# Local attention scores with one head per matmul: 64 rows by 32 columns, head halves interleaved on the partitions

## The chip, the cores and the metric

The kernel runs on one core of one Trainium2 chip. The metric is the device time in microseconds of one execution. The core has TensorE (PE, with its weight loads shown as PEld), VectorE (DVE), ScalarE (ACT), GpSimd (POOL) and SyncE (SP), which here only issues transfers.

## The reference

The input x is float32, 4 batch entries of 512 tokens with 128 features. Two sublayers follow each other, each with a residual and a layer norm at its end. The first is full attention with 16 heads of 8 features and an ALiBi bias. The second is a stack of six local layers, and the change is in their attention:

```python
for i in range(6):
    x = attn_layer(shift_tokens(x), Wqkv[i], q_scale[i], k_scale[i], Wo[i]) + x
    x = ffn_layer(shift_tokens(x), ln_g[i], ln_b[i], W1[i], b1[i], W2[i], b2[i]) + x
# attn_layer: 16 heads of 64 features; q and k are normalized, scaled and rotated
q = l2norm(q) * qs                     # the same for k
q = q * cos * scale + rotate_half(q) * sin * scale
# local_attention: windows of 32 queries; each sees its own window and the one before
sim = einsum('bhwie,bhwje->bhwij', bq, bk2) * 8.0      # bk2: 64 keys for each window
sim = where(mask, -max, sim)           # mask: j < i, or j > i + 32, or no such key
out = einsum('bhwij,bhwje->bhwie', softmax(sim), bv2)
```

`rotate_half` mixes feature d with feature d + 32 of a head, so a head's 64 features are held as two halves of 32. All work is float32.

## The kernel before

The program has four parts in sequence: the first attention (`alibi_attention`), a product of value and output weights for each head (`fold_values`), the six local layers (`local_layers`) and the last norm. The local layers take about three quarters of the time.

In `local_layers` a unit is one batch entry in one layer (24 units), and a unit has four quarters of four heads each (GH = 4), 96 quarters in all. Every engine runs the same loop `step(s)` over s, with its own part of the work written out in order by hand; semaphores join them. In step s the engines project and rotate k and q of quarter n = s, compute the scores of quarter c = s - 1, the exponentials of quarter d = s - 2, and weigh the rows of quarter e = s - 3; quarter h = s - 4 is projected out. Once per unit, spread over the steps, the feed-forward part runs: transposes, gate and linear matmuls (`first_half`, L902), GELU (L1015, with a table load at L1010 before it), the product hid (L1215), its second matmul (L986).

TensorE's order within one step is: k projection (L862), projection out (L881), q projection (L862), `weigh_rows` (L873), the sum over each head's features for k (L946), `scores` (L894), the same sum for q (L956), then the unit's feed-forward matmuls and transposes (L907).

The other engines follow. VectorE multiplies the projections by scale and rotation tables (L1135 to L1142), transposes the probabilities (L1156), floors the sums (L1178, L1196), sums the exponentials (den, L1181), inverts (rden, L1184), adds the mask to the scores (s_in, L1188 and L1190) and takes the row maximum (s_max, L1200). ScalarE squares the projections (L1026, L1031, L1037, L1039), takes the exponentials (L1001, 16 of 128x64 per step), copies the weighed rows zT out of PSUM (L997) and takes logarithm and exponential of the sums. POOL adds the squares (sumk, L1090; sumq, L1096), finishes the rotation in qfin and kfin (L1099, L1100, L1104, L1105), multiplies s_max by rq (lower, L1110) and normalizes the probabilities (L1078).

`qfin` and `kfin` hold on partition 32 hh + d the features d (index 0) and d + 32 (index 1) of head hh. The scores contract over 128 partitions, so transfers rearrange them: `qpair[:, p]` gets heads 2p and 2p + 1, each half of the features in one half of the partitions. `kpad` has the same rows but one copy for each of the two heads e, in which the other head's partitions stay zero; so one matmul of 128 rows gives both heads' scores for 32 queries and 2 x 64 keys. It has one leading window of zeros. The four windows w of a tile of 128 tokens go to PSUM partitions 32w to 32w + 31, that is to four 32-column strips of the array.

SyncE issues the transfers of quarter n in step s = n: four for `qpair` (L832) after `qfin_ok`, eight for `kpad` (L839) after `kfin_ok`, all behind a wait for the scores of quarter n - 1, then the rows `xk_prev` and the next weights. `bank_z` is PSUM of four banks: the scores use banks 0 and 1, which the weighed rows z of quarter e used before; hence the scores wait for `z01_ok`, the first of the two copies to zT. `pT` holds the transposed probabilities in the order t (tile of 128 tokens), then head; `rq` and `prob` use the same order.

## Time and profile before

| | us |
|---|---|
| median of 3 runs | 2041.87 |
| lowest and highest run | 2039.39, 2042.81 |
| the profiled execution, device time | 2042.99 |
| the profiled execution, span of the trace | 2040.9 |

The span runs from the first to the last instruction of the profiled execution; its device time is longer by 2.1 us. The profile was taken once, so durations from it are those of one execution. TensorE's mean granted clock is 0.968 of full speed over the span.

A group of rows names a source line, an engine, what is written and read, and the shapes. The x behind a group is its count. A float32 matmul of the program leaves two matmul and two weight load records. Idle time in brackets is that of the engine ahead of the instruction, with what ended it. Busy time of matmuls that run side by side counts once.

Loop steps repeat in a pattern of four, one unit. The rows below are taken from one such pattern, whose steps are called A (1013.83 to 1029.80 us, from one k projection to the next), B (to 1047.85), C (to 1063.96) and D (to 1078.07). By the code's order A has the gate matmuls, B the GELU and the linear matmuls, C the second matmul of the feed-forward part and D transposes and the norm's scaling.

### The profile page before, as it was taken

The page shows a single profiled execution, that of the slowest core. Times are in us where ns is not written, and L with a number is a line of the kernel's source. Part 1 is how long each engine was busy: PE and PEld are TensorE (multiplying, and loading weights), DVE is VectorE, ACT ScalarE, POOL GpSimd, SP SyncE. Part 2 cuts the span into 40 slices and gives each one's busy share as a digit, 9 for nine tenths or more (in the row PEclk, how much of TensorE's full clock was granted, in tenths as well). Part 3 has the DMA queues.
Part 4 walks back from the last instruction along what each step waited for, and adds up shares of the span by engine and source line. Part 5 has one row for each costly group of instructions (what it writes and reads, how often), then busy time and mean ns, then how long its engine had stood idle before and what let it go on. Part 6 is the DMA issues. An engine that isn't in the chain of part 4 may idle for free. (4 is left out here: it accounts for less than half of the span.)

```text
span 2040.9 us, 47434 instructions
## 1 busy us (share of the span) xinstructions
PE 1835.3 (90%) x18048; PEld 1023.9 (50%) x18048; DVE 1544.4 (76%) x2543; ACT 1383.9 (68%) x2862; POOL 1263.2 (62%) x1127
## 2 busy tenths in 40 slices
PE   5898898668999999999999999999999999999984
PEld 3443344524555555555555555555555555555541
DVE  4778886257877788788887888878887788877753
ACT  1454445237777777877778777778777877778851
POOL 4303300057877777777777787777877778777721
PEclk8899999769999999999999999999999999999996
DMA  9000000215323343233432234332343322233300
GB/s 192 2 2 1 2 2 2 63 46 98 75 69 75 81 89 75 68 71 82 87 80 69 68 81 86 74 79 68 75 88 74 83 68 69 67 77 84 71 22 21
DMA packets 142992, 131.86 MB, mean 65 GB/s; under 512 B 85160, under 2 KB 88808, under 8 KB 142440
## 3 DMA queue, kind: packets, MB, share of 16 engines
q1 hardware_dynamic: 142768, 128.83, 28.4%
q8 instruction: 145, 2.38, 0.5%
q14 instruction: 79, 0.65, 0.1%
HBM read 20.94 MB, written 1.05 MB: 11 GB/s over the span
## 5 line engine op out<-in xcount | busy, mean ns | idle before, releaser
L1001 ACT ACTIVATE prob<-s_in,lower,rq 128x64 f32<-128x64 f32 x1536 | 537.9, 430 | 79.0 <-POOL lower L1110 77.0
L862 PE MATMUL bank_a<-x_shift,wqk_sb 128*128 128x512 f32 x768 | 375.2, 612 | 69.1 <-ACT sq L1031 57.5
L881 PE MATMUL bank_y<-zT,wvo 128*128 128x512 f32 x768 | 345.2, 592 | 0.0
L1090 POOL TENSOR_TENSOR sumk<-sq 128x512 f32<-128x512 f32 x96 | 122.3, 1274 | 271.6 <-ACT sq L1031 271.6
L862 PEld LDWEIGHTS bank_a<-x_shift,wqk_sb 128*128 128x128 f32 x768 | 140.1, 193 | 262.0 <-issue 148.4
L881 PEld LDWEIGHTS bank_y<-zT,wvo 128*128 128x128 f32 x768 | 146.0, 190 | 183.7 <-issue 183.7
L894 PEld LDWEIGHTS bank_z<-kpad,qpair 128*32 128x32 f32 x6144 | 164.6, 110 | 100.1 <-issue 98.8
L894 PE MATMUL bank_z<-kpad,qpair 128*32 128x128 f32 x6144 | 187.7, 274 | 23.2 <-ACT zT L997 23.2
L491 DVE TENSOR_REDUCE a_negmax<-a_max 128x1 f32<-128x512 f32 x256 | 164.7, 685 | 47.9 <-PE a_max L166 44.3
L382 ACT ACTIVATE a_prob<-a_sT 128x1024 f32<-128x1024 f32 x128 | 130.5, 1023 | 103.7 <-PE a_sT L216 101.8
L997 ACT ACTIVATE zT<-bank_z 128x1024 f32<-128x1024 f32 x192 | 186.1, 1023 | 10.7 <-PE bank_z L873 8.0
L1078 POOL TENSOR_TENSOR prob<-prob,rden 128x1024 f32<-128x1024 f32 x96 | 182.9, 1905 | 3.9 <-DVE rden L1184 3.9
L1096 POOL TENSOR_TENSOR sumq<-sq 128x512 f32<-128x512 f32 x96 | 122.0, 1270 | 92.5 <-ACT sq L1039 92.5
L873 PE MATMUL bank_z<-pT,xk_prev 32*128 32x128 f32 x3072 | 164.8, 284 | 3.2 <-DVE xn L1162 1.7
L873 PEld LDWEIGHTS bank_z<-pT,xk_prev 32*128 32x128 f32 x3072 | 122.4, 187 | 78.4 <-issue 56.1
L873 PE MATMUL bank_z<-pT,xk_own 32*128 32x128 f32 x3072 | 154.8, 271 | 0.0
L1135 DVE SCALAR_TENSOR_TENSOR pk<-bank_a,scale_sb,rot_sb 128x512 f32<-128x512 f32 x96 | 71.8, 748 | 104.3 <-PE bank_a L862 94.3
L461 POOL TENSOR_TENSOR a_rstd<-a_mv,eps 128x4 f32<-128x4 f32 x4 | 0.8, 198 | 232.8 <-DVE a_mv L549 232.8
L1099 POOL TENSOR_TENSOR qfin<-pq 128x512 f32<-128x512 f32 x96 | 123.7, 1289 | 0.0
L873 PEld LDWEIGHTS bank_z<-pT,xk_own 32*128 32x128 f32 x3072 | 123.0, 188 | 0.0
L1141 DVE SCALAR_TENSOR_TENSOR pk<-bank_a,scale_sb,rot_sb 128x512 f32<-128x512 f32 x96 | 71.6, 746 | 67.6 <-ACT sq L1026 67.6
L1104 POOL TENSOR_TENSOR kfin<-rk,pk 128x512 f32<-128x512 f32 x96 | 122.1, 1272 | 0.5 <-ACT rk L1050 0.5
(161 smaller groups left out, 3947.3 us busy)
## 6 DMA issues: line engine op xcount, KB each, us to landing
qpair<-qfin SPq DMA_DIRECT2D x384, 128.0 KB, 2.3
kpad<-kfin SPq DMA_DIRECT2D x768, 64.0 KB, 2.0
wqk_sb<-in_wqkv SPq DMA_DIRECT2D x24, 256.0 KB, 5.6
xk_prev<-xk_own SPq DMA_DIRECT2D x24, 192.0 KB, 2.4
ffn_sb<-in_ffn SPq DMA_DIRECT2D x6, 537.5 KB, 3.9
wv_in<-in_wqkv SPq DMA_DIRECT2D x12, 256.0 KB, 4.8
wo_in<-in_wo SPq DMA_DIRECT2D x6, 512.0 KB, 5.8
xk_prev<-xk_own SPq DMA_DIRECT2D x24, 48.0 KB, 2.1
```

What stands on the lines that cost most here:

```text
L382: act.activation(prob[:, j % 2, 2 * half:2 * half + 2, :], sT_bank[:, 2 * half:2 * half + 2, :], ACT.Exp).then_inc(exp_ok, 1)
L491: dve.tensor_reduce(negmax[:, unit // 4, unit % 4:unit % 4 + 1], max_bank[u % 2][:], AX.X, ALU.max, negate=True).then_inc(max_ok, 1)
L862: last = pe.matmul(bank_a[:, half, :], wqk_sb[:, layer_of(u) % 2, part, half, g * P:(g + 1) * P], cols(u), start=True, stop=True)
L873: last = pe.matmul(bank_z[:, w, t * P:(t + 1) * P], rows[at, u % 2, t, :], pT[at, n % 2, c, t * GH:(t + 1) * GH, :].rearrange("p h q -> p ...
L881: last = pe.matmul(bank_y[:].rearrange("p (t w q) -> p t w q", w=WPT, q=WIN), wvo[:, layer_of(u), GH * g + hh, :], zT[:, n % 2, :, :, hh, ...
L894: last = pe.matmul(bank_z[WIN * w:WIN * w + WIN, t // 2, c:c + P], qpair[:, p, at:at + WIN], kpad[:, p, :, at:at + 2 * WIN], start=True, s ...
L997: return act.activation(out, in_, ACT.Copy)
L1001: last = act.activation(prob[:, n % 2, i, :], s_in[:, n % 2, i, :], ACT.Exp, bias=lower[:, n % 2, i:i + 1], scale=rq[:, n % 2, i:i + 1])
L1078: pool.tensor_tensor(prob[:, e % 2], prob[:, e % 2], rden[:].unsqueeze(2).broadcast_to([P, TPB * GH, 2 * WIN]), ALU.mult).then_inc(pn_ok, 1)
L1090: pool.tensor_tensor(sumk[:], sq[:, 0, :], sq[:, 1, :], ALU.add).then_inc(sumk_ok, 1)
L1099: pool.tensor_tensor(qfin[:, 0, :], pq[:, 0, :], pq[:, 1, :], ALU.subtract)
L1104: pool.tensor_tensor(kfin[:, 0, :], rk[:], pk[:, 0, :], ALU.mult)
```

## The change

The zero padding of heads goes away. `kpad` loses its head index; `qpair` and `kpad` get one head e on each half of the partitions, its two feature halves interleaved on even and odd partitions. Each score matmul takes one head: 64 rows by 32 columns and 64 keys, the two heads of a pair go to different banks. There are twice as many score matmuls with half the keys each. The order of heads in the scores, and so in `pT`, the sums for q and the masks, becomes head within pair, tile, pair; `weigh_rows` and `project_out` pick their columns accordingly. SyncE moves q and k by halves, two transfers each for the first and the second feature half, and the first half waits only for the first of POOL's two products (new semaphores `qfin0_ok`, `kfin0_ok`): eight transfers in place of twelve.

```diff
--- before.py
+++ after.py
@@ -739,7 +739,7 @@
         kfin = sb("kfin", [P, 2, L])
         qfin = sb("qfin", [P, 2, L])
         qpair = sb("qpair", [P, 2, L])
-        kpad = sb("kpad", [P, 2, 2, WIN + L])
+        kpad = sb("kpad", [P, 2, WIN + L])
         s_in = sb("s_in", [P, 2, TPB * GH, 2 * WIN])
         s_max = sb("s_max", [P, TPB * GH])
         lower = sb("lower", [P, 2, TPB * GH])
@@ -777,6 +777,7 @@
         sumk_ok, sumq_ok, rotk_ok, kfin_ok, qfin_ok, pn_ok, eps_ok, rstd_ok = map(
             sem, ["sumk_ok", "sumq_ok", "rotk_ok", "kfin_ok", "qfin_ok", "pn_ok", "eps_ok", "rstd_ok"])
         kpad_in, qpair_in, prev_in = sem("kpad_in"), sem("qpair_in"), sem("prev_in")
+        qfin0_ok, kfin0_ok = sem("qfin0_ok"), sem("kfin0_ok")
 
         def after(eng, s, n, each=1):
 
@@ -825,19 +826,17 @@
                     after(sp, xf_ok, B * layer + B - 1)
                     sp.dma_start(ffn_sb[:], ffn[layer + 1]).then_inc(ffn_loaded, 16)
                 if quarter(n):
-                    after(sp, qfin_ok, n)
                     after(sp, s_mm, n - 1)
-                    for p in range(2):
-                        for half in range(2):
-                            sp.dma_start(qpair[64 * half:64 * half + 64, p, :],
+                    for half, ok in ((0, qfin0_ok), (1, qfin_ok)):
+                        after(sp, ok, n)
+                        for p in range(2):
+                            sp.dma_start(qpair[half:P:2, p, :],
                                          qfin[64 * p:64 * p + 64, half, :]).then_inc(qpair_in, 16)
-                    after(sp, kfin_ok, n)
-                    for hh in range(GH):
-                        p, e = hh // 2, hh % 2
-                        for half in range(2):
-                            to = 64 * half + 32 * e
-                            sp.dma_start(kpad[to:to + 32, p, e, WIN:WIN + L],
-                                         kfin[32 * hh:32 * hh + 32, half, :]).then_inc(kpad_in, 16)
+                    for half, ok in ((0, kfin0_ok), (1, kfin_ok)):
+                        after(sp, ok, n)
+                        for p in range(2):
+                            sp.dma_start(kpad[half:P:2, p, WIN:WIN + L],
+                                         kfin[64 * p:64 * p + 64, half, :]).then_inc(kpad_in, 16)
                 u = rows_at(s)
                 if u is not None:
                     after(sp, xk_ok, u)
@@ -871,7 +870,7 @@
                         for w in range(WPT):
                             at = slice(WIN * w, WIN * w + WIN)
                             last = pe.matmul(bank_z[:, w, t * P:(t + 1) * P], rows[at, u % 2, t, :],
-                                             pT[at, n % 2, c, t * GH:(t + 1) * GH, :].rearrange("p h q -> p (h q)"),
+                                             pT[at, n % 2, c].rearrange("k (e t p) q -> k t e p q", e=2, t=TPB)[:, t],
                                              start=(c == 0), stop=(c == 1), skip_group_check=True)
                 last.then_inc(z_mm, 1)
 
@@ -879,7 +878,7 @@
                 u, g = divmod(n, GROUPS)
                 for hh in range(GH):
                     last = pe.matmul(bank_y[:].rearrange("p (t w q) -> p t w q", w=WPT, q=WIN),
-                                     wvo[:, layer_of(u), GH * g + hh, :],
+                                     wvo[:, layer_of(u), GH * g + 2 * (hh % 2) + hh // 2, :],
                                      zT[:, n % 2, :, :, hh, :].rearrange("p w t q -> p t w q"),
                                      start=(g == 0 and hh == 0), stop=(g == GROUPS - 1 and hh == GH - 1),
                                      skip_group_check=True)
@@ -889,12 +888,12 @@
                 for t in range(TPB):
                     for p in range(2):
                         for w in range(WPT):
-                            at = t * P + w * WIN
-                            c = (t % 2) * 2 * P + p * P
-                            last = pe.matmul(bank_z[WIN * w:WIN * w + WIN, t // 2, c:c + P],
-                                             qpair[:, p, at:at + WIN],
-                                             kpad[:, p, :, at:at + 2 * WIN], start=True, stop=True,
-                                             skip_group_check=True)
+                            for e in range(2):
+                                at, rows = t * P + w * WIN, slice(64 * e, 64 * e + 64)
+                                c = t * P + p * 2 * WIN
+                                last = pe.matmul(bank_z[WIN * w:WIN * w + WIN, e, c:c + 2 * WIN],
+                                                 qpair[rows, p, at:at + WIN], kpad[rows, p, at:at + 2 * WIN],
+                                                 start=True, stop=True, skip_group_check=True)
                 last.then_inc(s_mm, 1)
 
             def first_half(out, u, half, j):
@@ -945,7 +944,7 @@
                     after(pe, floorq_ok, n - 1)
                     pe.matmul(bank_f[:], same_head[:], sumk[:], start=True, stop=True).then_inc(sumk_mm, 1)
                 if quarter(c):
-                    after(pe, kpad_in, c, 128)
+                    after(pe, kpad_in, c, 64)
                     after(pe, qpair_in, c, 64)
                     after(pe, z01_ok, min(c - 2, QUARTERS - 1))
                     scores(c)
@@ -953,7 +952,7 @@
                     after(pe, sumq_ok, n)
                     after(pe, floor_ok, n)
                     for t in range(TPB):
-                        last = pe.matmul(bank_f[:, t * GH:(t + 1) * GH], sumq[:, t * P:(t + 1) * P], pick_head[:],
+                        last = pe.matmul(bank_f[:, 0:TPB * GH].rearrange("q (e t p) -> q t e p", e=2, t=TPB)[:, t], sumq[:, t * P:(t + 1) * P], pick_head[:],
                                          start=True, stop=True, skip_group_check=True)
                     last.then_inc(sumq_mm, 1)
                 if quarter(e):
@@ -1096,12 +1095,12 @@
                     pool.tensor_tensor(sumq[:], sq[:, 0, :], sq[:, 1, :], ALU.add).then_inc(sumq_ok, 1)
                     after(pool, pq_ok, n)
                     after(pool, qpair_in, n - 1, 64)
-                    pool.tensor_tensor(qfin[:, 0, :], pq[:, 0, :], pq[:, 1, :], ALU.subtract)
+                    pool.tensor_tensor(qfin[:, 0, :], pq[:, 0, :], pq[:, 1, :], ALU.subtract).then_inc(qfin0_ok, 1)
                     pool.tensor_tensor(qfin[:, 1, :], pq[:, 2, :], pq[:, 3, :], ALU.add).then_inc(qfin_ok, 1)
                     after(pool, rk_ok, n)
                     after(pool, rotk_ok, n)
-                    after(pool, kpad_in, n - 1, 128)
-                    pool.tensor_tensor(kfin[:, 0, :], rk[:], pk[:, 0, :], ALU.mult)
+                    after(pool, kpad_in, n - 1, 64)
+                    pool.tensor_tensor(kfin[:, 0, :], rk[:], pk[:, 0, :], ALU.mult).then_inc(kfin0_ok, 1)
                     pool.tensor_tensor(kfin[:, 1, :], rk[:], pk[:, 2, :], ALU.mult).then_inc(kfin_ok, 1)
                 if quarter(c):
                     after(pool, max_ok, c)
@@ -1116,7 +1115,7 @@
             pool.wait_ge(prev_zero, 1)
             for hh in range(GH):
                 pool.memset(same_head[32 * hh:32 * hh + 32, 32 * hh:32 * hh + 32], 1.0)
-                last = pool.memset(pick_head[32 * hh:32 * hh + 32, hh:hh + 1], 1.0)
+                last = pool.memset(pick_head[32 * hh:32 * hh + 32, 2 * (hh % 2) + hh // 2:2 * (hh % 2) + hh // 2 + 1], 1.0)
             last.then_inc(const_ok, 1)
             for s in range(STEPS_ALL):
                 step(s)
@@ -1189,7 +1188,7 @@
                                       mask_sb[:], ALU.add)
                     dve.tensor_tensor(s_in[:, c % 2, 8:16, :],
                                       bank_z[:, 1, :].rearrange("p (h n) -> p h n", n=2 * WIN),
-                                      mask_sb[:, 4:5, :].broadcast_to([P, 8, 2 * WIN]), ALU.add).then_inc(mask_ok, 1)
+                                      mask_sb[:], ALU.add).then_inc(mask_ok, 1)
                 if quarter(n):
                     after(dve, sumq_mm, n)
                     after(dve, lnq_ok, n - 1)
@@ -1222,7 +1221,7 @@
                     dve.scalar_tensor_tensor(hi, bank_z[64:P, 3, :], b2_sb[64:P], hi, ALU.add,
                                              ALU.add).then_inc(xf_ok, 1)
 
-            dve.memset(kpad[:].rearrange("p a b n -> p (a b n)"), 0.0).then_inc(kpad_zero, 1)
+            dve.memset(kpad[:].rearrange("p a n -> p (a n)"), 0.0).then_inc(kpad_zero, 1)
             dve.wait_ge(const_in, 16 * 18)
             for s in range(STEPS_ALL):
                 step(s)
@@ -1338,7 +1337,7 @@
     ok = (j >= i) & (j <= i + WIN)
     first = ok & ~((np.arange(P)[:, None] < WIN) & (j < WIN))
     low = np.float32(-(2.0 ** 100))
-    return np.stack([np.where(m, np.float32(0), low) for m in [first] * GH + [ok] * GH], 1).astype(np.float32)
+    return np.stack([np.where(m, np.float32(0), low) for m in [first] * 2 + [ok] * 6], 1).astype(np.float32)
 
 
 def three_parts(a):
```

## Rows read from the trace of the kernel before

**Rows 1.** Busy time of each engine over the span, part 1 of the page.
```profile
PE 1835.3 (90%) x18048; PEld 1023.9 (50%) x18048; DVE 1544.4 (76%) x2543; ACT 1383.9 (68%) x2862; POOL 1263.2 (62%) x1127
```

**Rows 2.** Busy time by windows: step B, and the sum over steps A to D.
```profile
1029.80:1047.85 18.05, 15.77 (x162) 8.72 (x160) 12.58 (x18) 14.09 (x31) 11.88 (x11) 1.00 0.26 60
...
sum 64.24, PE 61.34 PEld 35.22 DVE 52.22 ACT 50.19 POOL 49.06; mean PE 15.34 PEld 8.81 DVE 13.05 ACT 12.55 POOL 12.27
```

**Rows 3.** All waits of PE from 600 to 1900 us: total, times, longest.
```profile
PE bank_a L862 <- ACT sq L1031: 37.4, 20, 1.9
PE bank_z L894 <- ACT zT L997: 19.1, 81, 0.4
```

**Rows 4.** Windows, L894 alone: length, PE, PEld, clock, transfers.
```profile
1024.30:1024.40 0.10, 0.06 (x4) 0.09 (x8) 1.00 0.00 0
1024.30:1026.30 2.00, 1.96 (x64) 1.72 (x64) 1.00 0.00 0
```

**Rows 5.** Windows, L873 alone, the weighing of rows in step A.
```profile
1021.03:1021.06 0.03, 0.02 (x4) 0.02 (x4) 1.00 0.33 68
1021.03:1023.20 2.17, 2.07 (x64) 1.88 (x64) 1.00 0.45 125
```

**Rows 6.** Timeline around the scores in step B, then in step D.
```profile
1044.40 0.69 DVE L1188 TENSOR_TENSOR s_in<-bank_z,mask_sb 128x512 f32<-128x512 f32 x1 [0.28 <-PE bank_z L894]
...
1074.36 1.96 PE L894 MATMUL bank_z<-kpad,qpair 128*32 128x128 f32 x64 [0.18 <-ACT zT L997]
...
1076.07 0.25 DVE L1184 RECIPROCAL rden<-den 128x16 f32<-128x16 f32 x1
...
1076.38 0.69 DVE L1188 TENSOR_TENSOR s_in<-bank_z,mask_sb 128x512 f32<-128x512 f32 x1
```

**Rows 7.** Timeline from a step D into step A.
```profile
1008.90 1.27 POOL L1096 TENSOR_TENSOR sumq<-sq 128x512 f32<-128x512 f32 x1 [1.39 <-ACT sq L1039]
...
1015.05 0.23 POOL L1110 TENSOR_TENSOR lower<-s_max,rq 128x16 f32<-128x16 f32 x1
...
1018.46 0.58 ACT L1031 ACTIVATE sq<-bank_a 128x512 f32<-128x512 f32 x1
...
1019.12 0.30 PEld L862 LDWEIGHTS bank_a<-x_shift,wqk_sb 128*128 128x128 f32 x2 [0.81 <-ACT sq L1031]
```

**Rows 8.** Timeline at the end of step A and the start of B.
```profile
1028.33 1.28 ACT L1010 ACT_TABLE_LOAD   x1
...
1028.94 1.02 PE L902 MATMUL bank_f<-xnT,ffn_sb 128*85 128x512 f32 x2
...
1030.00 0.68 ACT L1015 ACTIVATE hid<-bank_f,ffn_sb 85x512 f32<-85x512 f32 x1 [0.39 <-PE bank_f L902]
```

**Rows 9.** Timeline at the start of step C.
```profile
1048.05 1.41 DVE L1215 SCALAR_TENSOR_TENSOR hid<-bank_z,ffn_sb,hid 128x512 f32<-128x512 f32 x2 [1.10 <-PE bank_f L902]
```

**Rows 10.** Timeline of VectorE from step C into step D.
```profile
1063.50 0.38 DVE L1209 BATCH_NORM_AGGREGATE mv<-stats 128x2 f32<-128x6 f32 x4
...
1064.16 0.74 DVE L1221 SCALAR_TENSOR_TENSOR x_shift<-bank_z,ffn_sb,x_shift 64x512 f32<-64x512 f32 x1 [0.28 <-PE bank_z L986]
...
1065.88 0.75 DVE L1135 SCALAR_TENSOR_TENSOR pk<-bank_a,scale_sb,rot_sb 128x512 f32<-128x512 f32 x1 [0.20 <-PE bank_a L862]
...
1069.68 1.32 DVE L1162 TENSOR_SCALAR xn<-bank_z,mv,rstd 128x128 f32<-128x128 f32 x4
...
1071.03 0.75 DVE L1135 SCALAR_TENSOR_TENSOR pq<-bank_a,scale_sb,rot_sb 128x512 f32<-128x512 f32 x1
```

**Rows 11.** Transfers: issues on the page, SP's wait, one timeline row.
```profile
qpair<-qfin SPq DMA_DIRECT2D x384, 128.0 KB, 2.3
kpad<-kfin SPq DMA_DIRECT2D x768, 64.0 KB, 2.0
...
SPq L784 <- PE bank_z L894: 581.4, 81, 9.9
...
1015.15 5.02 SPq L839 DMA_DIRECT2D kpad<-kfin  x8
```

## The prediction

> **What bounds the kernel now.** I read the page's busy shares first. TensorE is busy 90% of the span, far ahead of the other engines [rows 1], so a shorter block of matmuls could count. The busy share is an average, so I went to the local layers, where the change is. One loop step handles one quarter (four heads of one batch entry), and the four steps A to D repeat as a pattern of 64.24 us [rows 2]. TensorE is busy 61.34 of these 64.24 us at the full granted clock (1.00, 2.4 GHz). Its list of waits has two entries, over 81 steps: the q projection waits for ScalarE's Square in 20 of them, 37.4 us together, and the scores wait for the zT copy, 0.24 us each time [rows 3]. The reader should see that TensorE idles 2.9 us in 64 and nearly sets the pace, but that ScalarE already sets it in one step of four.
>
> **The score block itself.** It is 64 matmul records (a float32 matmul leaves two) and as many weight loads, 1.96 us busy, of which 1.72 us lie between the first and the last weight load [rows 4]. That is 0.1075 us for each four, one on each 32-column strip: 258 cycles of 2.4 GHz for 128 keys. So a strip takes two cycles for a key, and four strips run side by side. The block is bound by the columns that stream, not by issue. The weighting block shows the same for the other direction: 32-row tiles, 64 records in a stretch of 2.07 us busy, four of them started within 0.03 us [rows 5]. So tiles that differ in columns run together and tiles that differ in rows run together, in different banks.
>
> **The change, part by part.**
>
> *Half the columns, twice the matmuls.* Before, a matmul contracts 128 rows and computes two heads' keys, half of the products with padding zeros. After, 64 rows and 64 keys: 128 records, each with half the stream (0.054 us), on eight tiles (two row halves, four strips), whose order alternates halves, each half writing its own bank. If all eight run together the block is 128/8 x 0.054 = 0.86 us from first to last start, against 1.72. The tail behind the last start (1.96 - 1.72 = 0.24) shrinks by 0.05; against that, I allow 0.1 us for the first round, whose 16 instructions must arrive one by one. I take 1.16 us for the block, a gain of **0.80 us** per step on TensorE.
>
> *Can instructions arrive fast enough?* No stretch of this trace needs more than four pairs in 0.107 us for long. From above: in the first 0.10 us of the block eight loads and four matmuls had started, the first load 0.09 us before the window's end [rows 4]. Loads and matmuls alternate in the program, so the eighth load is the 15th instruction: 6 ns each at most. At 6 ns, 256 instructions take 1.54 us and the gain is 0.18 us. From below: 27 ns per pair, the average of both blocks, would be a floor if the chip issued matmuls no faster than that; the block would be 128 x 0.027 = 3.44 us, a loss of 1.72 us. The bursts [rows 4, 5] are the nearest evidence, four pairs in 0.03 us, so I take the fast case as likeliest.
>
> *Where the 0.80 us go.* The scores' end releases VectorE's masking (L1188). But VectorE does den and rden before it and ends them at 1076.32; the masking starts at 1076.38, and the scores ended at 1076.32 too [rows 6]. The two are level, in steps A, C and D; in B the masking waits 0.28 us. So masking, and the row maximum behind it, gain nothing. Only the matmuls behind the scores on TensorE's own queue start earlier. I follow each stretch from one q projection to the next.
>
> D to A: POOL runs without a gap from the sum for q (1008.90) over qfin and kfin to lower (1015.05), then ScalarE's exponentials and Squares run to 1019.04, and the q projection's weights, loaded from 1019.12, had waited 0.81 us for that Square [rows 7]. No score is in this chain. Gain **0**.
>
> A to B: the gate matmuls end earlier, but GELU needs its table first: the table load ends at 1029.61 and GELU started at 1030.00, released by TensorE [rows 8]. At most 0.39, less 0.05 of handover. ScalarE is then busy up to the next q projection. Gain **0.34**.
>
> B to C: the linear matmuls release VectorE's product for hid, for which it sat idle 1.10 us [rows 9]; everything up to the projection follows. Gain **0.80**.
>
> C to D: VectorE ends the aggregate at 1063.88 and its add (L1221) waited 0.28 us for TensorE. It can start 0.25 earlier, and the next product (L1135), which waited another 0.20 us for the k projection, 0.45 in all. From there VectorE runs without a gap up to xn, which ends at 1071.00, and the q products follow at 1071.03 [rows 10]. The projection gains 0.80, but what it releases gains 0.45. Gain **0.45**.
>
> Sum: 0.34 + 0.80 + 0.45 = 1.59 us in four steps. By the loop, GELU steps come every fourth step from step 11, 22 of them before the last quarter, so 22 such groups: 22 x 1.59 = **35 us**. In the first eight steps there is no feed-forward work, the chain of D to A rules, and I count nothing.
>
> *The transfers.* Eight instead of twelve issues per step, each of 64 partitions. They landed 2.0 and 2.3 us after issue [rows 11]. SP's queue waits 581 us for score matmuls in 81 steps, which is room, not cost. The last kpad issue ends at 1020.17 and the scores that read it start at 1024.3 [rows 4, 11], so the cover is 2 us even after landing. The first halves can start one POOL product (about 1.27 us) earlier and are behind the same wait for the previous scores. The new waits stand on SP alone, ahead of the next transfers and xk_prev, which also has slack. POOL's and VectorE's counts are unchanged, the signals ride on instructions that exist. Cost 0; if the cover were gone, a step would pay at most one landing, 2.3 us.
>
> *The rest.* Reordered columns of pT, wvo, pick_head and the masks, and the unbroadcast mask, keep the sizes; a strided stream of 64-column pieces was already the scores' form. Cost 0.
>
> **The sum.** The profiled run took 2042.99 us (span 2040.9 and 2.1 around it): 2042.99 - 35.0 = 2008.0. It lies 1.1 above the median of 2041.87, so I predict **2007 us**.
>
> **Rivals.**
>
> *1. Partly fed.* The stream of 256 instructions, not the array, sets the block: 6 ns each gives a gain of 0.18 us, worth 0.18 x 3 in four steps (A to B, B to C, C to D), 22 x 0.54 = 12 us: 2030 us. For it: the block starts behind a wait in every step [rows 3], so its instructions aren't all queued up. Against: it is an upper bound on the spacing. Anything between 2007 and 2030 belongs here.
>
> *2. Weight loads share a path.* If the four strips of a row half load one after the other at 0.027 us each (32 columns, two cycles), they take 0.107 us per eight, and the block stays at 1.72: no change, 2042 us. The present block can't exclude it by its average. Against: eight loads, two for each strip, started in 0.09 us [rows 4], where one path would give 0.22.
>
> *3. Issue bound, slower.* Matmuls are issued at a floor of 27 ns per pair in a long stream, the bursts being only what a full queue hands over. Then the block is 3.44 us, +1.72 on TensorE's own queue in each of 96 steps, 165 us: about 2207 us. For it: both blocks average 27 to 29 ns per pair, though one is tiled by rows and one by columns. Against: both have the same stream per tile and four tiles, which explains the same number. It decides from 13.4 ns per pair (1.72/128) upwards; at 18 ns, between that and 27, the block grows by 0.58 us and the kernel ends near 2098.
>
> The Trainium skill speaks for this rival: "TensorE: Matmul & The Clock Gate", in the section on 56 against 53.3 ns, says that starts of matmuls never come closer than about 25 ns however small they are. By that rule the block would be 128 x 0.025 = 3.2 us and the kernel, with +1.48 in 96 steps, would take about 2184 us. This trace shows starts within a burst closer than that, on different tiles, and an average just above it.
>
> *4. Clock.* With TensorE idle more, its clock could drop. It stays at 1.00 in B, where the idle wait is 1.87 us [rows 2, 3]; idle stretches grow by under 1 us. I give it nothing of its own.
>
> **Chances.** The fast case (2000 to 2015) 0.58; partly fed, 2015 to 2037, 0.10; no change, by rival 2 or a balance of both, 0.08; slower, 0.24, half of it below 2100. A change within 0.2% (4 us) can't be told from none. Faster 0.68, same 0.08, slower 0.24. The range runs from 1988, where the bounds by VectorE and POOL would be too strict and half as much again is gained, to 2098; about 0.14 lie outside. The likeliest case's own range is 1998 to 2015.
>
> **What would show it.** Right: a score block near 1.15 us with twice the records; the scores-to-masking gap opening by 0.8 us and masking released by rden; TensorE waiting for ScalarE in the q projection of A too; GELU released by its table load; step lengths that shrink by 0.8 in B to C and not in D to A; transfers with no waiter. Wrong: a block above 1.72 us with pair starts spaced evenly over it (rival 3), or rounds of eight at 0.107 us (rival 2); masking that does start earlier would make the gain larger than 35 us.

## The result, and the profile after

| | median, us | lowest to highest | runs |
|---|---|---|---|
| before | 2042.28 | 2039.39 to 2042.81 | 5 |
| after | 2029.19 | 2028.43 to 2030.77 | 5 |

The ratio is 0.994, with a 95% interval of 0.9926 to 0.9955: the kernel is 13.1 us faster. The forecast was 2007 us, a gain of 35. The sign is right, the gain is well under half of what I predicted, and the time lies outside the likeliest case's own range. The profiled execution took 2030.68 us, with a span of 2028.9 us and a mean granted clock of 0.963 (before 0.968).

New line numbers are one lower than those of before: the projections are L861, the scores still L894, the masking L1187, the Square L1030.

The page's busy times [rows 1], and the queue that fetches instructions. Its columns are packets, MB, and the share of 16 engines' span.

```profile
PE 1800.8 (89%) x24192; PEld 992.7 (49%) x24192; DVE 1529.0 (75%) x2543; ACT 1380.8 (68%) x2862; POOL 1262.7 (62%) x1127
```

```profile
q8 instruction: 194, 3.18, 0.6%
```

TensorE has 6,144 more matmul records and is busy 34.5 us less. The second line is one that I hadn't shown of before, where it reads 145 packets and 2.38 MB. Each packet is 16 KB. With its semaphore waits TensorE executes about 49,600 instructions where it executed 37,300, so there is about one packet to 256 of them.

Busy time by windows of the score block, L894 alone, in a step D (columns as in [rows 4], which show a block of step A; the block of step D before is in [rows 6]):

```profile
1074.50:1074.60 0.10, 0.05 (x8) 0.08 (x12) 1.00 0.00 0
1074.50:1076.10 1.60, 1.48 (x128) 1.34 (x128) 1.00 0.00 0
```

The block takes 1.48 us, where it took 1.96 and I had said 1.16. It gives each step 0.48 us, not 0.80.

The same view by steps, with all instructions: A, B and the sum over A to D, one pattern of four later than that of [rows 2]:

```profile
1077.78:1093.75 15.97, 15.29 (x226) 8.35 (x225) 12.28 (x17) 13.89 (x31) 13.58 (x12) 1.00 0.47 106
1093.75:1111.32 17.57, 15.30 (x225) 8.35 (x224) 12.43 (x18) 14.15 (x31) 11.88 (x11) 1.00 0.28 60
...
sum 62.81, PE 59.43 PEld 33.73 DVE 51.62 ACT 50.01 POOL 49.06; mean PE 14.86 PEld 8.43 DVE 12.90 ACT 12.50 POOL 12.26
```

Four steps shrank from 64.24 to 62.81 us. Between the q projections, as medians over the 22 groups, C to D went from 16.11 to 15.63, D to A stayed at 14.29, A to B went from 17.82 to 17.34, and B to C from 16.02 to 15.54: 0.48, 0, 0.48 and 0.48 us, together 1.44. Twenty-two times 1.44 is 31.7 us. Less than half of that reached the kernel's time: 13.1 us.

TensorE's waits from 600 to 1900 us show why (total, times, longest):

```profile
PE bank_a L861 <- ACT sq L1030: 45.1, 37, 1.9
PE bank_z L894 <- ACT zT L996: 19.3, 82, 0.4
PE bank_z L894 <- issue: 6.3, 3, 2.1
PE bank_z L906 <- issue: 2.6, 3, 1.1
PE bank_z L901 <- issue: 2.2, 2, 1.3
PE bank_f L955 <- issue: 1.6, 1, 1.6
```

The first two are those of [rows 3]. The Square is now waited for in 37 places, not 20. The four lines "issue" are new: time in which TensorE waited for nothing that the profile knows. Nine waits hold 12.7 us, and three of them are inside the score block. The timeline of one:

```profile
684.23 1.31 PEld L894 LDWEIGHTS bank_z<-kpad,qpair 64*32 64x32 f32 x125 [0.98 <-issue]
684.26 1.44 PE L894 MATMUL bank_z<-kpad,qpair 64*32 64x64 f32 x125 [0.18 <-ACT zT L996]
...
687.69 0.14 PEld L894 LDWEIGHTS bank_z<-kpad,qpair 64*32 64x32 f32 x3 [2.15 <-issue]
687.69 0.30 PE L894 MATMUL bank_z<-kpad,qpair 64*32 64x64 f32 x3 [1.99 <-issue]
...
688.03 0.69 DVE L1187 TENSOR_TENSOR s_in<-bank_z,mask_sb 128x512 f32<-128x512 f32 x1 [1.81 <-PE bank_z L894]
...
690.53 2.77 PE L861 MATMUL bank_a<-x_shift,wqk_sb 128*128 128x512 f32 x4
```

After 125 of its 128 pairs the block stops for 2.2 us, with everything that the last three read long in place. VectorE's masking stands idle for it, 1.81 us. And the projection behind it takes 2.77 us instead of 1.88. The windows show the reason, in the column of the granted clock:

```profile
684.20:685.50 1.30, 1.24 (x125) 1.27 (x125) 1.30 (x2) 1.30 (x2) 1.30 (x2) 1.00 0.05 13
685.50:687.65 2.15, 0.20 (x21) 0.04 (x5) 0.68 (x2) 0.67 (x2) 2.15 (x3) 1.00 0.00 0
687.70:690.50 2.80, 2.80 (x19) 2.71 (x20) 2.47 (x4) 1.03 (x3) 1.52 (x2) 0.71 0.46 99
690.50:693.30 2.80, 2.80 (x7) 1.29 (x6) 0.07 (x1) 2.45 (x7) 2.08 (x2) 0.68 0.95 206
```

The clock had been at 1.00 (2.4 GHz). After the gap it is granted 0.71 and 0.68, a mixture with 1.2 GHz, so the gap costs more than itself.

The same stretch in the transfer view, whose 40 slices are 0.125 us each:

```profile
GB/s 0 0 0 0 0 0 0 0 0 0 131 0 0 0 0 0 0 0 0 0 0 0 0 0 0 0 0 0 0 0 0 0 0 0 0 0 0 0 0 0
...
q8 instruction: 1, 0.02, 1.2%
```

The window is 684 to 689 us, and the one packet in it is an instruction packet: it begins in slice 11, at 685.35, 1.1 us into the block. By its record it takes 0.96 us, and TensorE goes on 1.38 us after its end.

Counting every TensorE instruction of the trace, waits included, I find eight gaps of over 1 us that no semaphore explains:

| quarter | 16 | 26 | 31 | 72 | 77 | 82 | 87 | 92 |
|---|---|---|---|---|---|---|---|---|
| gap, us, from start to start | 2.21 | 2.36 | 2.33 | 1.42 | 1.04 | 1.59 | 1.26 | 1.87 |
| place | in the block | in | in | behind it | behind | behind | behind | behind |

All eight begin at the same place of a 256-instruction grid: the first instruction behind the gap has a count that leaves 193 when divided by 256. They add up to 14.1 us. The stretches that they lie in, with the slower clock behind them, exceed the median of their kind by 20.2 us. And 31.7 - 20.2 = 11.5 us, against 12.0 by which the span became shorter. Of these 12.0, 1.4 lie ahead of the first q projection of the local layers, where the change does nothing, so the account closes to between one and two microseconds.

So two things had to be explained: the block's 1.48 us, and the gaps. My theory from here on: (a) the score block is bound by the arrival of its 256 instructions, 1289 ns from first to last start, or 5.0 ns each; (b) TensorE's instructions come in blocks of 256, and when 256 of them are used up faster than the next block can be fetched, TensorE stands still. The rivals: the array itself, or row halves that exclude each other, set the block; and the gaps belong to some event of those quarters (a weight reload, a busy port), not to the instruction count.

### The profile page after: what moved, and what is told of

Same layout as the page of the kernel before. It is cut to its first block and busy times, and to the rows that moved or that the text cites. A ratio compares the mean times of both kernels' runs of the same rounds, so it can differ in the third digit from the quotient of the medians.

```text
span 2028.9 us, 59338 instructions
## 1 busy us (share of the span) xinstructions
PE 1800.8 (89%) x24192; PEld 992.7 (49%) x24192; DVE 1529.0 (75%) x2543; ACT 1380.8 (68%) x2862; POOL 1262.7 (62%) x1127
## 5 line engine op out<-in xcount | busy, mean ns | idle before, releaser
L861 PE MATMUL bank_a<-x_shift,wqk_sb 128*128 128x512 f32 x768 | 377.5, 615 | 79.4 <-ACT sq L1030 68.2
L861 PEld LDWEIGHTS bank_a<-x_shift,wqk_sb 128*128 128x128 f32 x768 | 141.7, 195 | 273.3 <-issue 151.4
L894 PEld LDWEIGHTS bank_z<-kpad,qpair 64*32 64x32 f32 x12288 | 129.7, 105 | 107.5 <-issue 107.3
L1095 POOL TENSOR_TENSOR sumq<-sq 128x512 f32<-128x512 f32 x96 | 122.0, 1270 | 94.8 <-ACT sq L1038 94.8
L894 PE MATMUL bank_z<-kpad,qpair 64*32 64x64 f32 x12288 | 143.7, 225 | 29.6 <-ACT zT L996 23.2
L1098 POOL TENSOR_TENSOR qfin<-pq 128x512 f32<-128x512 f32 x96 | 123.5, 1287 | 0.0
L1099 POOL TENSOR_TENSOR qfin<-pq 128x512 f32<-128x512 f32 x96 | 122.3, 1274 | 0.0
```

Of the source, the lines that this page charges most:

```text
L861: last = pe.matmul(bank_a[:, half, :], wqk_sb[:, layer_of(u) % 2, part, half, g * P:(g + 1) * P], cols(u), start=True, stop=True)
L894: last = pe.matmul(bank_z[WIN * w:WIN * w + WIN, e, c:c + 2 * WIN], qpair[rows, p, at:at + WIN], kpad[rows, p, at:at + 2 * WIN], start=Tru ...
L1098: pool.tensor_tensor(qfin[:, 0, :], pq[:, 0, :], pq[:, 1, :], ALU.subtract).then_inc(qfin0_ok, 1)
L1099: pool.tensor_tensor(qfin[:, 1, :], pq[:, 2, :], pq[:, 3, :], ALU.add).then_inc(qfin_ok, 1)
```

## The experiments

Where no number of runs is given, a kernel was run once with a profile, beside a run of the kernel before on the same chip (2042.20 us).

**Half the streamed keys.** It computes only half of the scores (32 of 64 keys in each matmul), with the bank zeroed once; the number of instructions is the same.

```
-  last = pe.matmul(bank_z[WIN * w:WIN * w + WIN, e, c:c + 2 * WIN],
-                   qpair[rows, p, at:at + WIN], kpad[rows, p, at:at + 2 * WIN],
+  last = pe.matmul(bank_z[WIN * w:WIN * w + WIN, e, c:c + WIN],
+                   qpair[rows, p, at:at + WIN], kpad[rows, p, at:at + WIN],
   ...
+  dve.memset(bank_z[:, 0:2, :].rearrange("p w n -> p (w n)"), 0.0)
```

> The changed kernel, but each score matmul takes 32 of its 64 keys, so the stream of each is halved and the number of instructions stays 256 in a block. Half of the scores are left out. Changed kernel: 1.29 us from the first to the last start, 1.50 us busy. Theory 1 (instructions reach TensorE at about 5.0 ns each): the block keeps its 1.27 to 1.30 us between first and last start, and the time stays within 3 us of 2029. Theory 2 (the eight tiles hinder each other, 80 ns for a round of eight matmuls instead of 54): the stream sets the round, the block falls to 0.7 to 0.9 us and the time falls by 10 us or more.

It took 2044.08 us. Its group from 600 to 1900 us:

```profile
L894 PE MATMUL bank_z<-kpad,qpair 64*32 64x32 f32 x10368 | 105.9, 201 | 30.0 <-ACT zT L996 18.2 <-issue 11.8
```

With half the columns the block still needs 1118 ns from first to last start, against 1289: 4.4 ns an instruction. If the columns had set it, it would have halved. But it isn't untouched either: I had expected 1270 to 1300, so the columns have a share of 171 ns, and the arrival of instructions alone doesn't explain the block. The four steps take 62.36 us, 0.45 less than the change's. Yet the time is 15 us worse. There are now 11 gaps, 22.0 us, in stretches that are 35.8 us too long, and five more stretches, without a gap, are 7.0 us too long, because the granted clock fell in them. The faster block uses its instructions up sooner: in quarter 16 the gap starts after 1.08 us of the block and lasts 2.57. My forecast of the time didn't have that.

**Row halves one after the other.** Only the order of the loops differs, so 64 pairs use four tiles and then 64 the other four.

```
-  for t in range(TPB):
-      for p in range(2):
-          for w in range(WPT):
-              for e in range(2):
+  for e in range(2):
+      for t in range(TPB):
+          for p in range(2):
+              for w in range(WPT):
```

> The changed kernel, but all score matmuls of one row half come first and then all of the other, so only four tiles are in use at a time. Nothing else differs. If the two row halves really run side by side in the changed kernel, four tiles with a round of 0.054 us give 128/4 x 0.054 = 1.72 us from first to last start, as before the change, and the time goes back toward 2042. If the halves never overlapped, or if the arrival of instructions alone sets the block, it stays at 1.29 us and 2029.

It took 2075.94 us, and its group from 600 to 1900 us reads:

```profile
L894 PE MATMUL bank_z<-kpad,qpair 64*32 64x64 f32 x10112 | 149.8, 217 | 26.7 <-ACT zT L996 18.5 <-issue 8.2
```

The block needs 1692 ns from first to last start, which is that of four tiles (16 x 107 = 1.72 us). The change's block is shorter than that, so its row halves do run together, and that is where its whole gain is. Four steps take 64.00 us. That the kernel is nevertheless 34 us slower than before is for the most part again the gaps: 9 of them, 14.3 us, in stretches that are 30.3 us too long. Before, 128 instructions took 1.72 us, here 256 do: it isn't the shorter block that brings the gaps, but the larger number of instructions.

Another 10 us are six stretches of 1.7 us too much each that hold no gap. The windows around one of them, ahead of and behind the moment in question:

```profile
905.00:907.90 2.90, 2.79 (x137) 2.73 (x137) 2.87 (x5) 2.02 (x3) 2.90 (x4) 1.00 0.03 6
908.00:911.40 3.40, 3.40 (x5) 1.27 (x5) 1.56 (x3) 1.81 (x3) 3.40 (x4) 0.51 0.78 171
```

TensorE had been busy 2.79 of 2.90 us, with scores and the sum for q, and the granted clock falls from 1.00 to 0.51 all the same. So a wait isn't needed for it; what it takes I can't say.

**Half of the block.** It leaves out the scores of the second half of the query tiles, so each step has 128 instructions fewer; the bank is zeroed once as above.

```
-  for t in range(TPB):
+  for t in range(TPB // 2):
```

> The changed kernel without the score matmuls of the last two of the four token tiles: 64 of 128, half of the scores left out. The block should be 0.65 us between starts. Theory of the prediction (VectorE and POOL set the pace next): D to A stays 14.29 us; A to B and C to D keep the 0.48 us they had gained, within 0.15; B to C falls by another 0.6; with no late instruction fetches the time is about 1995. Rival (TensorE's queue sets the pace throughout): all three stretches fall by 0.6 each, the pattern of four steps is 60.9 us, and the time is about 1969.

It took 2005.71 us, with no gap. The block is 663 ns long, 0.85 us busy. This asks the question that the change was too slow to ask: what would the rest of the kernel make of a really short block? Neither theory came out (1995 and 1969 us). Against before, C to D gained 1.10 us where I had expected 0.48, and D to A lost 0.21, so 0.89 together; A to B gained 0.57. B to C, which should have fallen by another 0.6, gained only 0.18 on average: one stretch of three gained 1.11, and the other two are 0.24 us longer than before. The timeline of the q projection at the start of such a longer stretch, and windows before it and over it, say why:

```profile
1022.16 3.53 PE L861 MATMUL bank_a<-x_shift,wqk_sb 128*128 128x512 f32 x4 [2.40 <-ACT sq L1030]
```

```profile
1016.00:1022.00 6.00, 3.75 (x9) 1.33 (x7) 2.81 (x5) 5.97 (x14) 1.24 (x1) 0.99 0.32 70
1022.16:1025.70 3.54, 3.54 (x8) 1.22 (x8) 2.27 (x3) 2.53 (x8) 3.54 (x3) 0.55 0.00 0
```

TensorE has waited 2.40 us for the Square, longer than the 1.9 us of before, and the granted clock falls from 0.99 to 0.55. The projection takes 3.53 us instead of 1.88, and gives the whole gain of that stretch back. This is my rival 4, which I had given nothing. In the change itself the longest such wait between 600 and 1900 us is 1.9 us, and there the clock fell only behind gaps.

**The count moved by 40.** Ten small matmuls ahead of TensorE's loop, 40 instructions of about 50,000, into a bank that is written afterwards. Nothing in the loop changes but its place on the grid of 256.

```
+  for _ in range(10):
+      pe.matmul(bank_f[0:32, 0:4], ident[0:32, 0:32], ident[0:32, 0:4],
+                start=True, stop=True)
   pe.wait_ge(const_ok, 1)
   for s in range(STEPS_ALL):
```

> The changed kernel with 40 more TensorE instructions (ten matmuls of 32x32 by 4) ahead of its loop, while TensorE waits for POOL anyway. In the changed kernel TensorE ran dry at one place of the score blocks of quarters 16, 26 and 31 (2.2 to 2.4 us each) and a little later in those of 72, 82, 87 and 92; each place is 192 more than a multiple of 256 TensorE instructions. Theory 1 (instructions come in blocks of 256, and a block is asked for too late when the block before is used up in 1.3 us): the gaps leave quarters 16, 26 and 31 and appear in other blocks, in the series 12, 17, 22, 27, 32, always 192 above a multiple of 256. Theory 2 (a transfer or another engine's timing at those moments): the gaps stay in quarters 16, 26 and 31.

It took 2052.59 us, 23 more than the change. TensorE's waits, 600 to 1900 us:

```profile
PE bank_a L861 <- ACT sq L1032: 45.2, 36, 1.9
PE bank_z L894 <- ACT zT L998: 18.9, 80, 0.4
PE bank_z L894 <- issue: 14.0, 7, 2.3
PE bank_f L955 <- issue: 6.3, 4, 2.0
```

The block (1287 ns) and the four steps (62.80 us) are as in the change; the waits for ScalarE are the same too. The gaps are now 13, in quarters 7, 12, 17, 22, 27, 32, 37, 42, 47, 57, 62, 67 and 93, and the three quarters that stopped inside their block in the change (16, 26, 31) run free. All 13 are again at the same place of the grid. The rival that some event in those quarters makes the gap is refuted: the gap follows the count. The account closes again, to a few microseconds: 31.9 us gained by the steps, 41.9 lost in stretches with gaps, together 10.0 slower than before, and 10.4 was measured, although the part ahead of the local layers was 2.9 us faster.

**The count steered.** If the gaps are only a matter of where a block of 256 begins, they can be led away. This one puts 16 small matmuls ahead of the loop, and 11 more in each of four steps, before the sum of k, where the grid would drift back onto the scores.

```
+  for _ in range(11 if n in (34, 50, 66, 82) else 0):
+      pe.matmul(bank_f[0:32, 0:4], ident[0:32, 0:32], ident[0:32, 0:4],
+                start=True, stop=True)
   pe.matmul(bank_f[:], same_head[:], sumk[:], start=True, stop=True)
   ...
+  for _ in range(16):
+      pe.matmul(bank_f[0:32, 0:4], ident[0:32, 0:32], ident[0:32, 0:4],
+                start=True, stop=True)
```

> The changed kernel with dummy matmuls (32x32 by 4, four instructions each) that only move the place of the score blocks in TensorE's instruction stream: 16 ahead of the loop, and 11 ahead of the sum for k in steps 34, 50, 66 and 82. With them no score block from the eighth on starts between 167 and 209 above a multiple of 256, the places at which the blocks of the changed kernel and of shift40 ran dry. Theory 1 (a block of 256 instructions is asked for too late when it is used up in 1.3 us): no gap over 0.3 us inside or right behind a score block is left, the pattern of four steps stays 62.81 us, and the time falls by the 20 us that the late steps add, to 2008 to 2013. Theory 2 (the gaps come about once in so many blocks wherever these stand): gaps of 2 us remain and the time stays at 2025 or above.

| | median, us | lowest to highest | runs |
|---|---|---|---|
| before | 2041.85 | 2038.51 to 2044.69 | 13 |
| steered | 2014.86 | 2013.83 to 2016.57 | 4 |

The ratio to before is 0.9872 (0.9858 to 0.9887): 27.0 us faster than before, about 14 faster than the change. TensorE's waits in the same stretch:

```profile
PE bank_a L861 <- ACT sq L1034: 45.4, 36, 2.0
PE bank_z L894 <- ACT zT L1000: 18.6, 79, 0.4
PE bank_z L906 <- issue: 1.9, 4, 0.7
```

The four steps still take 62.81 us, and no gap is over 1 us. What remains are four waits of up to 0.7 us, in quarters 28, 44, 76 and 92, again at the one place of the grid; I had expected none over 0.3, but the stretches that they lie in are no longer than the median. The cure has its own price: the four A-to-B stretches with 11 more matmuls are 3.0 us longer in all, and in the stretch behind the last of them, after a wait of 2.0 us for the Square, the granted clock fell to 0.50 and cost another 1.4. That is why the time is just above the expected 2013. It is the version that beats both kernels.

**The transfers alone.** The kernel before, with its 12 transfers signalled by halves, so that the first half of qfin and of kfin goes out one POOL product earlier.

```
-  pool.tensor_tensor(qfin[:, 0, :], ...)
+  pool.tensor_tensor(qfin[:, 0, :], ...).then_inc(qfin0_ok, 1)
   ...
-  pool.tensor_tensor(kfin[:, 0, :], ...)
+  pool.tensor_tensor(kfin[:, 0, :], ...).then_inc(kfin0_ok, 1)
   # and on SP's queue, the same for kfin0_ok and kfin_ok
-  after(sp, qfin_ok, n)
   after(sp, s_mm, n - 1)
+  for half, ok in ((0, qfin0_ok), (1, qfin_ok)):
+      after(sp, ok, n)
+      # the transfers of this half
```

> The kernel before the change with one part of it alone: the transfers of qpair and kpad go by halves, the first half after the first of POOL's two products (twelve transfers as before, score matmuls as before). My theory: no engine waits for them, so 2042 within 2 us. Rival: transfers that start earlier let the scores or POOL go on earlier, and part of the 13 us comes from here: 2038 or less.

It took 2041.74 us (2039.68 to 2043.25, 10 runs) against 2041.85, ratio 0.9998 (0.9988 to 1.0008). Earlier transfers are worth nothing, within the measurement's grain. The eight larger transfers of the change weren't run by themselves.

## Why the prediction came out as it did

**The block's size (mis-sized).** The step "I take 1.16 us for the block, a gain of 0.80" is the term that was off: 1.48 us and 0.48. The mechanism was right as far as it went: both row halves do run side by side, since in turn they take 1.69 us. But they don't reach the 0.86 us of eight full tiles, and the best account that I have is that the instructions can't come fast enough to keep them busy. The windows of [rows 4] held the answer, in the figure that I used only as a bound: 6 ns an instruction at most. Measured are 5.0 over the whole block. It isn't even: the first 32 pairs or so start about 7.3 ns apart, a burst, and from there on each instruction takes about 5.5 ns. What a short burst shows is not the average of 256. My rival 1, partly fed, was the right one for the block, between its own bounds. That the kernel's 2029 lies in its 2007 to 2030 as well is luck: with 0.48 us a step rival 1 gives 3 x 22 x 0.48 = 31.7 us, about 2010, and the rest came from the gaps, which it doesn't have.

**Where the gain goes (nearly right).** D to A gained 0, as predicted. B to C gained all of the block's 0.48. The two caps were too low: A to B, which I capped at 0.34, gained the full 0.48, and with shorter blocks 0.55 and 0.57; C to D, capped at 0.45, gained 0.48, and with shorter blocks 0.67 and 1.10. One reason is my step on the masking, "masking gains nothing". The timeline after, in step D (the row of L894 is also the block of the windows above):

```profile
1074.55 1.48 PE L894 MATMUL bank_z<-kpad,qpair 64*32 64x64 f32 x128 [0.18 <-ACT zT L996]
...
1076.26 0.25 DVE L1183 RECIPROCAL rden<-den 128x16 f32<-128x16 f32 x1
1076.43 0.63 DVE L1187 TENSOR_TENSOR s_in<-bank_z,mask_sb 128x512 f32<-128x512 f32 x1
```

The scores end at 1076.03 and the masking starts 0.40 us later, so the scores no longer release it, as I had said. But it starts 0.17 us after rden's start, where it had been 0.31 [rows 6]: the two had not been level, the masking had waited some 0.13 us for the scores in A, C and D, and that is what it gained there (0.36 in B). The Square's release of the projection, in A, has appeared where the matmul had not waited before, as I had said it would:

```profile
1083.59 1.95 PE L861 MATMUL bank_a<-x_shift,wqk_sb 128*128 128x512 f32 x4 [0.49 <-ACT sq L1030]
```

GELU did not change hands. The three rows that answer to [rows 8]:

```profile
1092.56 1.28 ACT L1009 ACT_TABLE_LOAD   x1
...
1092.89 1.02 PE L901 MATMUL bank_f<-xnT,ffn_sb 128*85 128x512 f32 x2
...
1093.95 0.68 ACT L1014 ACTIVATE hid<-bank_f,ffn_sb 85x512 f32<-85x512 f32 x1
```

GELU starts 0.04 us after the gate matmul's end (1093.91), as it did before, and 0.11 after the table load's, which had been 0.39. The table load itself comes 0.21 us earlier after A's q projection (8.97 us, before 9.18), because the masking and the sums behind it do. So the cap was 0.39 + 0.21 less the handover, not 0.34; with the half block GELU does start at the table load's end, and there the stretch gains 0.57.

With the measured block and the measured stretches, the sum would have been 1.44 x 22 = 31.7 us: two errors, a block gain of 0.48 instead of 0.80 and caps too strict, that nearly cancelled against my 35.

**The term that was missing.** "Can instructions arrive fast enough?" asked for the spacing within the block, and not for what brings the instructions. That is the failed step of the sum: it has no term for the next 256. Every gap of over 1 us that is counted above, in this kernel and in the experiments, ends in the same way. The last instruction packet takes 0.9 to 1.4 us, and TensorE goes on 1.2 to 1.7 us after its end, with a median of 1.4. The packet itself begins 0.9 to 3.0 us behind the preceding point of the grid. From one point to the next that makes at least 3.1 us where TensorE had to stop, although it had used the 256 instructions up in 1.2 to 3.4 us. In the kernel before, the fastest 256 TensorE instructions in a row, wherever they begin, take 4.9 us; with half the block they take 3.9; neither kernel has such a gap. In the change they take 1.3. Doubling the score instructions has put the stream into the range where it can run dry, and the places where it can are the points of the grid, which are arithmetic of the program and not of its data. The place alone doesn't decide: in quarter 21 a grid point falls as deep into the block as in quarter 26 (247 and 248 instructions), and TensorE paused 0.23 us there and 2.36 here. What differs is the packet, which began 0.6 us behind the preceding point in the one and 2.6 in the other. In the change, wherever 256 instructions between two points passed in under 3.5 us with no pause over 0.3, the packet had begun at most 0.8 us behind the first. The gaps cost 20.2 us here and 41.9 with 40 instructions more in front; the steered kernel has none, and loses about 5 us to the steering itself.

The Trainium skill has the structure of it, in "Advanced Engine Details and Errata", section "ISA Cache": instructions are held in lines of 16 KB, which it counts as 256 instructions. The trace agrees, with 194 packets of 16 KB and every gap at one place of a grid of 256. The section of the Trainium skill on issue spacing that I quoted in the prediction ("TensorE: Matmul & The Clock Gate"), of starts never under 25 ns apart, doesn't hold for matmuls on different tiles: 128 pairs started 10.1 ns apart.

**The rivals.** 2 (a shared path for weights) and 3 (a floor of 27 ns for a pair) are both refuted by 10.1 ns per pair, and 2 also by the experiment with the halves apart. 4 (the clock) was wrongly given nothing: at 0.71 and 0.68 behind a gap, it makes gaps of 2.2 to 2.4 us into losses of 3.3 to 5.8. Behind the other five gaps, of 1.0 to 1.9 us, 0.65 to 2.8 were lost.

**The transfers.** Cost 0 fits the last experiment and the change's trace, in which TensorE waits for no transfer between 600 and 1900 us. SP's room is still there but stands elsewhere: it waits 802 us in 82 places for POOL's first product and 9.7 us for the scores, where it had waited 581 for the scores [rows 11].

**What stays open.** The trace shows when an instruction packet moves, not what asks for it. Why it begins 0.9 us behind a grid point in one place and 3.0 in another, while some blocks of 256 pass without a stop in 2.8 us, and one even in 1.35, with its packet begun 1.0 us ahead of the point, and what fills the 1.4 us between its end and the next instruction, I can't say. That the block's 5.0 ns an instruction are the arrival of instructions rests on the keys experiment (half the columns, 13% less time) and on the halves (four tiles alone need 1.69 us); I didn't measure the supply by itself. A tile handles a pair every 80 ns in the change, every 70 with half the keys, and every 53 when the halves go in turn, so a load and the stream behind it on one tile don't simply add up; but some other cost of eight tiles at once isn't excluded. Each kernel was profiled in one execution, so the gaps are those of one execution each.

## What to carry to other kernels

When a change multiplies small instructions, cost them as a stream: 5 ns for each of a long row here, loads counted too, and not only what the array does with them. Then look for the fastest 256 instructions in a row on that engine. The kernels here in which they take 3.9 and 4.9 us had no gap, and those in which they take 1.1 to 1.7 had 8 to 13, except the one that was steered; in between nothing was measured. In such a kernel the engine may stand still at places that move whenever anything ahead of them adds or drops an instruction, so read the waits marked "issue" before two such versions are compared. A few idle instructions in front of the loop are the test for it, and, well placed, they are the cure, at a small price of their own.

## What I had not expected of the hardware

- Matmuls with their weight loads on eight tiles start 10.1 ns apart over a run of 128 pairs, and about 7 ns apart at its beginning; halving the columns only takes that to 8.8.
- TensorE stands for up to 2.6 us when its instructions run out, and the packet that it waits for is 16 KB and 1 us long; 40 idle instructions in front of the loop move the whole kernel from 2029 to 2053 us, and 60 idle matmuls, well placed, move it to 2015.
- Behind a gap of 2.2 us the granted clock was 0.71, behind a wait of 2.40 us it was 0.55, and behind one of 2.0 us in the steered kernel 0.50; in the change's step whose projection waits 1.86 us it is 1.00 throughout. With the row halves in turn it fell to 0.51 with no wait in front at all.
